# One core, attention and experts in one kernel: new places for steps in the prologue and around the last attention unit

## What is computed

```python
mod = (silu(c) @ wmod).reshape(4, 6, 1, 256)          # sa, ca, ga, sb, cb, gb
h = layernorm(x) * (1 + ca) + sa
k, q, v = per head: W_K h, W_Q h, W_V h               # 16 heads, width 128
z = softmax(causal(q k^T) / sqrt(128)) v
x = x + ga * (W_O z)                                  # ga, gb kept away from zero
h = layernorm(x) * (1 + cb) + sb
u = h @ down_w + down_b
probs = softmax(h @ router_w + router_b - cost);  two best, softmax of the two
out = sum over the two of gate * (gelu(gelu(u masked) @ w1 + b1) @ w2 + b2), 8 experts of 128 to 512
out = (out + 0.1 * shared(u)) @ up_w + up_b + gelu(h) @ core_w + core_b
x = x + gb * out
```

## Time and profile before

| | us |
|---|---|
| median of three runs | 813.04 (811.65 to 814.38) |
| the profiled execution | 812.05 |
| its span, first to last instruction | 810.0 |
| PE busy / weight loads / DVE / ACT / GpSimd | 784.7 / 700.6 / 679.5 / 628.4 / 441.2 |
| mean granted TensorE clock | 0.996 |

### The profile page before, as it was taken

One profiled execution on the slowest core, in us unless ns is written; L12 is line 12 of the kernel. 1 busy time (PEld: TensorE's weight loads), 2 busy tenths in 40 slices (PEclk: granted clock), 3 DMA queues, 4 the chain that ended last, 5 costly groups with the idle time before them and its releaser, 6 DMA issues.

```text
span 810.0 us, 14461 instructions
## 1 busy us (share of the span) xinstructions
PE 784.7 (97%) x4806; PEld 700.6 (86%) x4806; DVE 679.5 (84%) x1649; ACT 628.4 (78%) x1417; POOL 441.2 (54%) x305
## 2 busy tenths in 40 slices
PE   7899899999999999999999999999999989989997
PEld 6789898999999999999999999999999767778786
DVE  4789998888888888888888888889898989887967
ACT  3787878877887788877778888877778968876974
POOL 2555365654456655445566544576545474577654
PEclk9999999999999999999999999999999999999999
DMA  7262233343222444322344332244332230111231
GB/s 264 64 171 68 63 90 93 91 104 86 66 66 66 101 108 108 83 66 66 72 104 106 91 92 66 66 97 115 94 76 60 64 105 34 67 58 66 69 102 53
DMA packets 47593, 70.54 MB, mean 87 GB/s; under 512 B 5536, under 2 KB 38464, under 8 KB 47392
## 3 DMA queue, kind: packets, MB, share of 16 engines
q1 hardware_dynamic: 47008, 68.81, 32.4%
q0 software_dynamic: 368, 0.81, 0.3%
q10 hardware_dynamic: 144, 0.00, 0.0%
HBM read 25.49 MB, written 2.17 MB: 34 GB/s over the span
## 4 chain that ended last, share of the span: by engine, by line
PE 64%; ACT 17%; DVE 11%; issue 5%; POOL 2%; DMA 1%; SPq 0%; DVEq 0%; POOLq 0%
PE M L732 10%; PE M L733 9%; PE M L731 9%; PE T L731 7%; PE T L733 7%; PE T L732 7%; PE S L731 5%; PE S L733 5%; PE S L732 5%; ACT PB L623 4%; ACT PB L672 3%; ACT pth L699 2%; DVE S L1135 2%; ACT qk L685 2%; ACT hh L665 1%
## 5 line engine op out<-in xcount | busy, mean ns | idle before, releaser
L623 ACT ACTIVATE PB<-S,nb 128x128 f32<-128x128 f32 (+3 forms) x256 | 133.9, 533 | 109.9 <-DVE nb L1135 109.9
L580 POOL TENSOR_TENSOR ptl<-ptl,pth 128x640 fp32r<-128x640 f32 x126 | 196.8, 1584 | 31.9 <-ACT pth L699 31.9
L573 POOL TENSOR_TENSOR X<-X,fb 128x512 f32<-128x512 f32 x64 | 83.1, 1299 | 239.5 <-DVE fb L1172 239.5
L672 ACT ACTIVATE PB<-PB,ri 128x256 f32<-128x256 f32 (+3 forms) x256 | 124.5, 580 | 6.4 <-DVE ri L1144 6.3
L1135 DVE CUSTOM_DVE_ANT_0 S<-S,cc 128x128 f32<-128x128 f32 (+3 forms) x256 | 117.6, 523 | 1.3 <-PE S L733 1.3
L1124 DVE TENSOR_TENSOR qk<-M,qk 128x512 fp32r<-128x512 f32 x108 | 74.6, 691 | 45.0 <-ACT qk L685 45.0
L1151 DVE STREAM_TRANSPOSE gab<-PB 128x256 f32<-128x256 f32 (+2 forms) x192 | 109.4, 623 | 0.0
L731 PE MATMUL S<-qk 128*128 128x128 f32 (+3 forms) x256 | 86.6, 338 | 4.6 <-DVE qk L1124 4.6
L699 ACT CAST pth<-ptl 128x640 fp32r<-128x640 f32 x128 | 87.8, 745 | 1.1 <-DMA ptl<-gab 1.1
L731 PE MATMUL M<-hh,W 128*128 128x512 f32 x222 | 86.7, 390 | 0.5 <-DVE hl L1110 0.5
L732 PE MATMUL M<-hl,W 128*128 128x512 f32 x222 | 86.5, 390 | 0.0
(11 more groups left out here) (255 smaller groups left out, 2410.7 us busy)
## 6 DMA issues: line engine op xcount, KB each, us to landing
ptl<-gab SPq DMA_DIRECT2D x256, 160.0 KB, 3.0
stage<-in_wat SPq DMA_DIRECT2D x16, 512.0 KB, 5.0
gab<-scw SPq DMA_DIRECT2D x16, 256.0 KB, 3.2
tmp<-scw SPq DMA_DIRECT2D x16, 256.0 KB, 3.6
X<-in_x SPq DMA_DIRECT2D x3, 512.0 KB, 8.3
stage<-in_wfa SPq DMA_DIRECT2D x3, 512.0 KB, 4.5
out<-X SPq DMA_DIRECT2D x3, 512.0 KB, 2.7
X<-in_wmod SPq DMA_DIRECT2D x1, 1024.0 KB, 11.8
```

The costliest lines, as they stand in the source:

```text
L573: pool.tensor_tensor(X[:, a:a + 512], X[:, a:a + 512], fb[:, c2 * 512:c2 * 512 + 512], ALU.add).then_inc(s_y, 1)
L580: pool.tensor_tensor(ptl[u % 2][:, s], ptl[u % 2][:, s].bitcast(F32), pth[u % 2][:, s].bitcast(F32), ALU.subtract).then_inc(s_pl, 1)
L623: ins = act.activation(PB[:, P_OFF[i]:P_OFF[i] + w], PS[bk][:, a:a + w], ACT.Exp, bias=nb[:, i:i + 1], scale=-1.0, accum_out=sm[:, i:i + 1])
L672: act.activation(p, p, ACT.Copy, scale=ri[:, i:i + 1]).then_inc(s_P3, 1)
```

## The change

Prologue: the 16 warm-up matmuls behind `mod` go. In the plan k(0) stands ahead of the first two statistics steps of batch 1, and a new event `ob` behind them takes over two small DVE instructions that `mg` had; `mg` is read out by ACT, and v(0,0) is placed behind S(1). PE alone follows another order for three events: q(1) ahead of S(0), v(0,0) ahead of S(1), q(3) ahead of S(2); since q's high half overwrites what S reads, ACT waits for S there. `ms` moves from the end of iteration 0 to behind v(1,0), ahead of z(0). The two halves of batch 3's `h` move from the ends of iterations 6 and 7 into iteration 7, behind wo and behind v.

Around the last unit: `pt` of unit 62 goes ahead of the router's start; of the router's steps 3 to 9 only 3 to 5 stay ahead of the experts, and the rest follow behind chunks 0, 1 and 3; piece 22 (`wh`) goes from chunk 4 to behind r(1) at chunk 5; the second half of batch 2's normalisation goes ahead of dn(1); steps 10 to 14 of batch 2's router go to chunks 18 and 19.

```diff
--- before.py
+++ after.py
@@ -20,7 +20,7 @@
 LAG = 4
 FIRST_ACC = 6
 EULER = 2.718281828459045
-WARM = 60, 16, 12
+WARM = 60, 0, 12
 INV = 1.0 / float(DH) ** 0.5
 BIG = 3.0e38
 
@@ -52,7 +52,7 @@
     def put(where, i, *events):
         where.setdefault(i, []).extend(events)
 
-    put(post, 0, ("ms",))
+    fill[0] = [[], [], [("ms",)]]
     for b in (1, 2, 3):
         i = (0, 2, 5)[b - 1]
         if b == 1:
@@ -61,8 +61,11 @@
             continue
         fill[i] = [[("st", b, 0)], [("st", b, 1)], [("st", b, 2)], [("st", b, 3)]]
         fill[i + 1] = [[("nm", b, 0)], [("nm", b, 1)]]
-        put(post, i + 1, ("h", b, 0))
-        put(post, i + 2, ("h", b, 1))
+        if b == 2:
+            put(post, i + 1, ("h", b, 0))
+            put(post, i + 2, ("h", b, 1))
+        else:
+            fill[i + 2] = [[], [], [("h", b, 0)], [("h", b, 1)]]
     for n in range(4, 16):
         put(pre, 16 * (n // 4 - 1) + 5 + 2 * (n % 4), ("wh", n))
     for n in range(16, 20):
@@ -76,9 +79,9 @@
     plan = [("mod0",)] + [("st", 0, k) for k in range(4)] + [
         ("silu",), ("nb", 0), ("nm", 0, 0), ("nm", 0, 1), ("mod",), ("wh", 0), ("ld", 2),
         ("h", 0, 0), ("h", 0, 1), ("wh", 1), ("ld", 3),
-        ("q", 0), ("st", 1, 0), ("st", 1, 1), ("k", 0), ("wh", 2), ("ld", 4), ("S", 0), ("st", 1, 2), ("st", 1, 3),
-        ("q", 1), ("ri", 0), ("k", 1), ("norm", 0), ("nb", 1), ("ty", 0), ("nm", 1, 0), ("nm", 1, 1), ("v", 0, 0),
-        ("mg",), ("tr", 0), ("S", 1), ("q", 2), ("ri", 1), ("k", 2), ("norm", 1), ("ty", 1), ("pt", 0), ("mh",), ("v", 0, 1),
+        ("q", 0), ("k", 0), ("st", 1, 0), ("st", 1, 1), ("ob",), ("wh", 2), ("ld", 4), ("S", 0), ("st", 1, 2), ("st", 1, 3),
+        ("q", 1), ("ri", 0), ("k", 1), ("norm", 0), ("nb", 1), ("ty", 0), ("nm", 1, 0), ("nm", 1, 1),
+        ("mg",), ("tr", 0), ("S", 1), ("v", 0, 0), ("q", 2), ("ri", 1), ("k", 2), ("norm", 1), ("ty", 1), ("pt", 0), ("mh",), ("v", 0, 1),
         ("wh", 3), ("tr", 1)]
     loads = {0: [5]}
     for i, events in pre.items():
@@ -104,8 +107,8 @@
         plan += [ev for group in steps for ev in group]
         plan += post.get(i, [])
     u = NU - 1
-    plan += [("S", u), ("wo", u // 2 - 2, 1), ("v", u // 2, 1), ("ex", u), ("ri", u), ("r", 0), ("rs", 0, 1),
-             ("rs", 0, 2), ("pt", u - 1), ("ra",), ("wx", u // 2 - 2, 1), ("b1",)] + [("rs", 0, k) for k in range(3, 10)] + [
+    plan += [("S", u), ("wo", u // 2 - 2, 1), ("v", u // 2, 1), ("ex", u), ("ri", u), ("pt", u - 1), ("r", 0),
+             ("rs", 0, 1), ("rs", 0, 2), ("ra",), ("wx", u // 2 - 2, 1), ("b1",)] + [("rs", 0, k) for k in range(3, 6)] + [
              ("dn", 0), ("z", u - 2)]
     return plan + [("norm", u), ("ty", u), ("tr", u), ("z", u - 1), ("ld", 22)]
 
@@ -129,17 +132,17 @@
             put(rest[0], j, ("rs", b, k))
         put(*weights, ("wt", b))
 
-    put(0, 0, ("rs", 0, 10), ("rs", 0, 11), ("rs", 0, 12))
-    put(0, 1, ("wo", last - 1, 0), ("rs", 0, 13), ("rs", 0, 14))
+    put(0, 0, ("rs", 0, 6), ("rs", 0, 7), ("rs", 0, 8), ("rs", 0, 9))
+    put(0, 1, ("wo", last - 1, 0), ("rs", 0, 10), ("rs", 0, 11), ("rs", 0, 12))
     put(0, 2, ("wo", last - 1, 1), ("wh", 21))
-    put(0, 3, ("pt", NU - 1))
-    put(0, 4, ("wx", last - 1, 1), ("wh", 22))
+    put(0, 3, ("pt", NU - 1), ("rs", 0, 13), ("rs", 0, 14))
+    put(0, 4, ("wx", last - 1, 1))
     put(0, 6, ("wt", 0), ("wl", 0), ("wl", 1), ("wl", 2), ("d0", 0))
     put(0, 7, ("z", NU - 1), ("st", 6, 0), ("st", 6, 1), ("d0", 1))
     put(0, 8, ("wo", last, 0), ("st", 6, 2), ("st", 6, 3), ("d0", 2))
     put(0, 9, ("wo", last, 1), ("wl", 3), ("nb", 6))
     put(0, 10, ("nm", 6, 0))
-    put(0, 11, ("dn", 1), ("nm", 6, 1))
+    put(0, 11, ("nm", 6, 1), ("dn", 1))
     put(0, 12, ("h2", 2, 0))
     put(0, 14, ("h2", 2, 1), ("st", 7, 0))
     put(0, 15, ("st", 7, 1), ("st", 7, 2))
@@ -149,13 +152,14 @@
     put(0, 19, ("nm", 7, 1))
     put(0, 20, ("dt",))
     router(1, ((0, 5), (0, 6), (0, (11, 11, 11, 12, 12, 14, 14, 15, 15, 15, 16, 16))), (0, 19))
+    put(0, 5, ("wh", 22))
     put(1, 1, ("h2", 3, 0))
     put(1, 3, ("D", 1))
     put(1, 4, ("h2", 3, 1))
     put(1, 5, ("D", 0), ("hs", 0, 0))
     put(1, 7, ("gx", 0, 0), ("hs", 0, 1))
     put(1, 9, ("gx", 0, 1))
-    router(2, ((1, 6), (1, 8), (1, (14, 14, 14, 15, 15, 16, 16, 17, 17, 17, 18, 18))), (2, 0))
+    router(2, ((1, 6), (1, 8), (1, (14, 14, 14, 15, 15, 16, 16, 18, 18, 18, 19, 19))), (2, 0))
     router(3, ((2, 4), (2, 5), (2, (11, 11, 11, 12, 12, 14, 14, 15, 15, 15, 16, 16))), (2, 19))
     for t in range(1, B):
         first = t == 1
@@ -639,6 +643,10 @@
                     if piece_after(n):
                         act.wait_ge(mf, use[piece_after(n)] + 1)
                     act.copy(wt(slot, a, w)[0], stage[:, (n % 2) * 1024:(n % 2) * 1024 + w]).then_inc(s_wh, 1)
+                elif kind == "mg":
+                    act.wait_ge(mf, use[ev] + 1)
+                    act.wait_ge(me, use[ev])
+                    act.copy(fb[0:4, 0:512], bank(ev)[0:4, :]).then_inc(me, 1)
                 elif kind == "nm" and ev[1:] in ACT_NM:
 
                     _, n, k = ev
@@ -673,6 +681,8 @@
                 elif kind in ("q", "k", "v", "z"):
                     act.wait_ge(mf, use[ev] + 1)
                     if kind == "q":
+                        if ev[1] in (1, 3):
+                            act.wait_ge(s_S, 3 * ev[1])
                         dst = qk[:, 0:512]
                     elif kind == "k":
                         dst = qk[:, 1024:1536]
@@ -740,7 +750,11 @@
 
             warm(WARM[0])
             ln_no = 0
-            for ev in plan:
+            order = list(plan)
+            for u, ev in ((0, ("q", 1)), (1, ("v", 0, 0)), (2, ("q", 3))):
+                order.remove(ev)
+                order.insert(order.index(("S", u)), ev)
+            for ev in order:
                 kind = ev[0]
                 if kind in MISC:
                     m = use[ev]
@@ -1037,13 +1051,11 @@
                     v.wait_ge(s_mod, 1)
                     v.tensor_copy(modt[:, 0:8], PS[0][:, 0:8])
                     v.tensor_scalar(modt[:, 8:16], PS[0][:, 8:16], 1.0, None, ALU.add).then_inc(s_mc, 1)
-                elif kind == "mg":
+                elif kind == "ob":
                     v.wait_ge(s_b, 48)
                     v.wait_ge(s_bc, 16)
                     v.tensor_tensor(oub[:], oub[:], gab[:, 0:256], ALU.add).then_inc(s_ob, 1)
                     v.tensor_scalar(bc[:, B_SH2:B_SH2 + 1], bc[:, B_SH2:B_SH2 + 1], 0.1, None, ALU.mult).then_inc(s_ob, 1)
-                    v.wait_ge(mf, use[ev] + 1)
-                    v.tensor_copy(fb[0:4, 0:512], bank(ev)[0:4, :]).then_inc(me, 1)
                 elif kind == "ms":
                     v.wait_ge(mf, use[ev] + 1)
                     v.tensor_copy(modt[:, 16:24], bank(ev)[:, 0:8])
```

## The result

The changed kernel takes 818.98 us (median of 5, 816.93 to 819.87), the kernel before beside it 812.70 (811.01 to 814.38): a ratio of 1.0063 with an interval of 1.0044 to 1.0083, 6.3 us slower. I had forecast 812.6 us and a range up to 816.0: wrong in sign and outside the range. The profiled execution has a span of 816.7 us (before 810.0).

A forecast was written before the change was run, and what follows sets the result against it. PE, busy 97% of the span, was taken as the bound, with DVE setting the pace in the hand-over. Terms -2.2 + 0.6 + 2.5 - 1.0 - 0.3 = -0.4 us took the median 813.04 to 812.6 us, range 808.4 to 816.0.

The forecast's parts named there:

- (e): Batch 3's layer norm, both halves in one unit: first wait disappears, second grows to 1.8 us; +0.6 us.
- (f): Hand-over to the experts: unit 62's low half ahead of the router's first steps makes w1(0) 1.6 us later.
- (g): Router steps 6 to 9 moved behind w1(0), where DVE is full; with (f) +2.5 us, bounds -1.4 and +3.1.
- (h): Batch 2's second half normalised on ACT ahead of the down projection's two gelus removes a PE wait; -1.0 us.
- (i): Batch 2's router, steps 10 to 14 placed later: wait moved to `wt`, not removed; -0.3 us.
- (a): Prologue without the 16 warm-up matmuls: q(0), k(0) and S(0) come 1.0 us earlier.
- (b): Prologue, k(0)'s low half ahead of two statistics steps, q(1) ahead of S(0): S(0) at 19.55 instead of 20.56 us.
- the clock stays low: Rival, chance 0.12: without warm-ups the prologue's clock rises later, +0.3 in place of -2.2 us; 815.1 us.
- (c): Prologue, gate's matmuls earlier, its copy on ACT, v(0,0) evicted later: S(2) 2.2 us sooner, at 34.75.
- (d): Prologue, shift matmuls `ms` ahead of z(0): the lead of 2.2 us is kept to q(4), at 49.8.
- DVE's queue costs more: Rival, chance 0.12: router step 14 later than w1(3)'s low half delays PE before `wt`; +3.1 us, 816.1 us.

The follow-up runs named there:

- o1: Kernel before with only the edits at the hand-over from attention to experts, router 0's steps 6 to 14 at their old places; 814.76 us, ratio 0.9999.
- n2: The change with the steps of batch 2's router where they were before; 817.24 us, ratio 1.0058.
- e1: Kernel before with only the prologue's edits and those of batch 3; ratio 0.9997.
- n4: Kernel before with only batch 2's second normalisation ahead of dn(1) and piece 22 behind r(1); ratio 0.9997.
- e2: Kernel before with only the edits at the hand-over from attention to the experts; median 816.77 us, ratio 1.0036.
- e3: Kernel before with only steps 10 to 14 of batch 2's router moved to chunks 18 and 19; ratio 0.9995.
- o2: Kernel before with small matmuls that nobody reads ahead of q(8), z(62), z(63) and w1(42); 813.25 us, ratio 0.9992.
- o3: Kernel before with the prologue's and batch 3's edits, but `ob` behind S(0)'s masks on DVE; 812.15 us, ratio 0.9972.
- e4: Kernel before with the prologue's and batch 3's edits, but the 16 warm-up matmuls kept; ratio 1.0003.
- n3: The change with 24 small matmuls ahead of w1(0) and of the transposing matmuls of routers 0 and 2; 815.69 us, ratio 1.0036.
- q1: Kernel before with the prologue's edits, `ob` behind S(0)'s masks, batch 2's second normalisation ahead of dn(1), piece 22 behind r(1); 810.43 us, ratio 0.9960.
- the built version with filled waits: q1 with small matmuls in the waits ahead of q(8), z(62), z(63) and w1(42); on the last chip 807.93 us, ratio 0.9930.

## Why the prediction was wrong

The terms, forecast and as the profile after shows them: prologue and (e) -1.6, came as -0.8; (f) and (g) +2.5, came as +4.8; (h) -1.0, came as -0.2; (i) -0.3, came as +1.1; and three that the sum didn't have, -1.6 and +0.5 at 705 and 723 and +2.8 at half clock. But for rounding that adds up to the +6.7 of the table, in place of -0.4. The largest miss on a term that the sum had is (g).

**Prologue, forecast -2.2, measured -0.76 at q(4).** (a) and (b) gave S(0) at 19.55; it came at 20.40. The weights landed 0.28 us later than in the trace of before, and q(0) ran at 1.2 GHz, since the clock was low for 6.8 us from 10.5 us on (before 3.4 us from 11.5). That isn't the missing warm-ups: o1, which has them, had 6.8 us too, from 9.3 us. Where q(0) was not slowed, S(0) came 10.5 us (n2) and 10.6 (e1) behind the first matmul on those weights, against 11.7 before: (a) and (b) at their forecast 1.0, though the old prologue itself gave 11.4 to 12.2 in other kernels (n4, e2, e3, o2). My rival *the clock stays low* named a risk that is there in either kernel. (c) was forecast at 1.2 us from S(0) to S(2) and gave 0.6. The term that failed in the prologue is `ob` at 0.41: its row had no GpSimd addition beside it, and I had looked for new neighbours at the moved steps of (g), not at this one. (d), the lead kept to q(4), was right. (e) was forecast at +0.6 and cost 0.15 (-0.8 at 91 us to -0.65 at 140): waits of 0.21, 0.45 and 0.87 us took the place of 0.22 and 1.02, each smaller than the 1.8 that I had put into one.

**(f), right in mechanism.** Forecast w1(0) +1.6, e2 shows +1.7. Inside the change it was +2.7: unit 62's transfer landed late (the ACT row above waits 1.18 us for it; before, ACT had no such wait). SP's four issues of that transfer took 3.8 us in the change, 3.6 and 3.7 in e1 and o3, and 2.6 in the kernel before and in e4. It is the second issue, 1.3 to 1.9 us in place of 0.6, in the eight kernels that lack the 16 warm-ups and put no small matmuls into a wait before it, and in no other; why, stays open. So taking the warm-ups out went with up to 1.0 us at w1(0), a part of what no part of the change has alone.

**(g), the step that failed.** (f) and (g) together were put at +2.5, bounds -1.4 and +3.1. From 629 to 661 e2 lost 3.6 us and the change 4.8. The mechanism is the one of the rival *DVE's queue costs more*, which had a chance of 0.12 and 816.1 us, still 2.9 short of the result: the wait for step 14 ahead of `wt` was 2.30 us (3.14 in e2). I had written "1 to 2 us" without following the row to its end. I had priced steps 6 to 9 (1.5, measured 1.4) and only named the place of steps 13 and 14, behind w1(3)'s low half; the four instructions that this puts ahead of them are 3.4 us, the largest part of the 8.7. The 0.7 that I had taken off for piece 22 came (0.68 us in place of 1.43), but behind `wt`, where it can't shorten this wait, while two of the moved steps, beside GpSimd, paid 1.9 us more than their 0.19 of before. The Trainium skill's rule that I had named in the forecast was the better guide there, with more for each new neighbour than the 0.7 that I had worked out.

**(h), forecast -1.0, is about 0.** -1.2 at h2(2,0), +1.0 by 674, in every kernel that has it. The wait moved, a case that I had named for (i) and not for (h).

**(i), forecast -0.3.** u's low half did come ahead (wait 0.21 in place of 2.07) and the wait did move to `wt`, but 1 us longer: the ratio alone is that of no change, and the 1.8 us inside the change are not clear of noise.

**What no step had.** The sum held PE's idle time and DVE's lateness and no clock outside the prologue. The stretch behind router 2 cost the change 2.8 us, against 1.6 of the kernel before at 698, and n3 shows by 3.3 us of the medians that the loss goes when the waits are filled. The seventeen profiles bear this out at router 2 (ahead of w1(42) or of `wt`): of the eleven that wait 2.3 to 3.1 us there, ten have a half-clock stretch that begins within 1.2 us of the wait's end, e3 alone doesn't; of the six that wait 2.13 us or less, none has one. But the parts have such waits alone too (e1 3.05 us, e2 2.50 and 3.14, e3 2.82), so why parts worth +1.8 us became +6.3 together is answered only in part: by the late transfer of unit 62, and by 2.8 us at half clock where e1 alone lost 1.3 and e2 and e3 none. And where a stretch falls isn't settled by waits alone: the kernel before had one at 698 us with no idle time above 0.23 us near it, n2, n3, e3, o1 and q1 one between 88 and 98 us where others had none.

## What to carry to other kernels

Before a step is moved out of a hole in a saturated engine's queue, find the matmul that waits for the last step of its row, not only for the first, and add up everything that comes to stand ahead of that step; here a few router steps cost 4.4 us. Price each moved VectorE step by what GpSimd runs at its new time: the same addition was 0.42 and 1.75 us, and moving one event was worth 1.3 us of the whole in medians (e1 less o3, on two chips) and 1.8 us from S(0) to S(2) (e1's 16.14 less 14.3). On a PE-bound kernel count a long wait with the half clock that may follow, and where it can't be removed, try small matmuls in it: 2.5 and 3.3 us here, though on the kernel before the 0.9 us are within the noise.

## What the runs showed of the hardware that I had not expected

A stretch of 3.4 us at the granted clock of 0.5 cost 1.3 to 1.6 us where PE was the bound (the kernel before from 697.6 on: 1.57) and nothing in the end where it fell ahead of a wait for DVE, as in e2 and e3 at 38 to 41 us and in the change at 638. Executions of one kernel differ by it: the kernel before took 812.26 us at a mean clock of 0.996 and 816.80 at 0.989. On the last chip its times lay between 811.27 and 816.91 us and those of the built version with filled waits between 806.76 and 808.45, less than a third of that spread.
